# Softmax shift of half the head units on TensorE, own banks for the last pair, and a new step table

## The reference

```python
k, q, v = heads(LN-free context, LN(x), context)       # 16 heads of 8 features
score = einsum('bhij,bhkj->bhik', k, q) / sqrt(8)
attn = softmax(score, axis=1)                          # over the 16 heads
x = x + tanh(g) * (einsum('bhik,bhij->bhjk', attn, v) ... @ Wo.T + bo)
x = x + tanh(g) * moe(LN(x))                           # 8 experts of 256, top 2, silu(x w0) * (x w1) @ wo
z = concat([c, c2q, c * c2q, c * q2c]) @ W_l.T + b_l   # second attention, c = LN(x), q = context
x = x + tanh(g) * z
x = x + tanh(g) * bitlinear_ffn(LN(x))                 # 128 -> 512 -> 128, gate, up and down
```

## Time and profile before

| what | us |
|---|---|
| median of 3 runs (lowest, highest) | 435.32 (432.39, 439.3) |
| the profiled execution | 432.61 |
| its span | 430.8 |
| busy PE, DVE, POOL, ACT | 317.4, 328.7, 285.2, 238.5 |

### The profile page before, as it was taken

One profiled execution on the slowest core, in us unless ns is written; L12 is line 12 of the kernel. 1 busy time (PEld: TensorE's weight loads), 2 busy tenths in 40 slices (PEclk: granted clock), 3 DMA queues, 4 the chain that ended last, 5 costly groups with the idle time before them and its releaser, 6 DMA issues. The chain is left out here.

```text
span 430.8 us, 9908 instructions
## 1 busy us (share of the span) xinstructions
PE 317.4 (74%) x3106; PEld 275.4 (64%) x3106; DVE 328.7 (76%) x1003; ACT 238.5 (55%) x630; POOL 285.2 (66%) x440
## 2 busy tenths in 40 slices
PE   0133348889888888898998898878879978984622
PEld 0122236778787777777887797768768867873501
DVE  1467445968778999999899989997989877785233
ACT  3503314534574679468847865785558647645434
POOL 4145877788889698789869897888686934231100
PEclk9999999999899999999999999999999999996555
DMA  5672410430141024003400430034000100100000
GB/s 169 187 201 71 115 59 2 118 92 2 41 123 48 2 68 138 6 0 88 135 4 2 124 97 2 2 98 114 3 11 2 38 2 2 38 2 1 12 0 12
DMA packets 34214, 24.03 MB, mean 56 GB/s; under 512 B 3570, under 2 KB 31860, under 8 KB 34164
## 3 DMA queue, kind: packets, MB, share of 16 engines
q1 hardware_dynamic: 33444, 23.22, 18.9%
q10 hardware_dynamic: 720, 0.20, 0.2%
HBM read 16.07 MB, written 7.34 MB: 54 GB/s over the span
## 5 line engine op out<-in xcount | busy, mean ns | idle before, releaser
L816 PE MATMUL ps_z<-m_xhi,w_hi 128*128 128x256 f32 x256 | 81.1, 317 | 14.9 <-DVE m_h L1141 8.3
L620 POOL TENSOR_TENSOR attn<-attn,head_inv 128x1024 f32<-128x1024 f32 x32 | 75.7, 2369 | 2.3 <-DVE head_inv L1116 2.3
L698 ACT ACTIVATE m_tanh<-ps_z 128x256 f32<-128x256 f32 x128 | 48.6, 383 | 46.7 <-PE ps_z L818 46.6
L817 PE MATMUL ps_z<-m_xhi,w_lo 128*128 128x256 f32 x256 | 73.2, 286 | 0.0
L1009 PE MATMUL ps_d<-wdn,m_h 128*128 128x128 f32 x512 | 70.8, 281 | 3.3 <-DVE m_h L1141 1.3
L818 PE MATMUL ps_z<-m_xlo,w_hi 128*128 128x256 f32 x256 | 73.1, 285 | 0.0
L1009 PEld LDWEIGHTS ps_d<-wdn,m_h 128*128 128x128 f32 x512 | 62.2, 191 | 6.7 <-issue 3.0
L567 POOL TENSOR_TENSOR m_h<-m_u,m_z 128x256 f32<-128x256 f32 x56 | 41.1, 735 | 37.6 <-DVE m_u L1133 37.6
L1133 DVE SCALAR_TENSOR_TENSOR m_u<-m_tanh,ps_z 128x256 f32<-128x256 f32 x128 | 53.1, 415 | 15.0 <-ACT m_tanh L698 13.4
L816 PEld LDWEIGHTS ps_z<-m_xhi,w_hi 128*128 128x128 f32 x256 | 49.5, 193 | 22.1 <-DVE m_u L1133 8.7
L614 POOL TENSOR_TENSOR tree<-tree 128x256 f32<-128x256 f32 (+2 forms) x96 | 48.5, 505 | 7.5
(11 more groups left out here) (205 smaller groups left out, 762.2 us busy)
## 6 DMA issues: line engine op xcount, KB each, us to landing
rows_dram<-qk_parts SPq DMA_DIRECT2D x16, 192.0 KB, 2.1
k_rows<-rows_dram SPq DMA_DIRECT2D x16, 192.0 KB
q_rows<-rows_dram SPq DMA_DIRECT2D x16, 192.0 KB
w_raw<-in_w SPq DMA_DIRECT2D x2, 1024.0 KB, 6.8
rows_dram<-qk_parts SPq DMA_DIRECT2D x16, 128.0 KB, 1.8
x_in<-in_x SPq DMA_DIRECT2D x8, 128.0 KB, 2.2
ct_in<-in_ctx_t SPq DMA_DIRECT2D x8, 128.0 KB, 2.3
rows_dram<-qk_parts SPq DMA_DIRECT2D x16, 64.0 KB, 1.9
```

The source lines that it names most:

```text
L620: pool.tensor_tensor(e, e, head_inv[:, u % 2].unsqueeze(1).to_broadcast([P, HEADS, HALF]), ALU.mult).then_inc(s_attn, 1)
L698: act.activation(m_tanh[:, k % 2], ps_z[k % 2][:, 0:TOK], ACT.Tanh, scale=0.5).then_inc(s_mt, 1)
L816: pe.matmul(dst, hi_w, hi_x, start=start, stop=False)
L817: pe.matmul(dst, lo_w, hi_x, start=False, stop=False)
```

## The change

The step table gets one time for each step and pair (`WHEN`), and the set-up of weights becomes steps of their own (`ONCE`). In units 1 and 3 of every pair (`PE_UNITS`) the shift goes to PE: after the maximum, ACT and DVE split it in a high and a low part of 128x64, PE multiplies them by minus the identity into both banks of `ps_sc` (four matmuls of 512 columns, each part read as 8 copies), and computes the scores a second time on top; ACT takes the exponential right from `ps_sc`. In the first pair two units sum their heads by one DVE reduction (`SUM_DVE`). The biases are three bf16 parts on partitions 0, 32 and 64, prepared once. `ct_hi`, `ct_lo`, `g_tanh` and `g_u` have two buffers. The k projection comes before the transposes of x. The products `f_z` are two steps; in the last pair the second batch's go to `ps_a`, each `g_up` unit has its own bank, and the second batch's transposes and `g_down` go to `ps_d`. The high parts of w0 and w1 are made in halves, as four steps on ACT.

```diff
+PE_UNITS = {c: (1, 3) for c in range(PAIRS)}
+SUM_DVE = {0: (1, 3)}
...
-AT = {
...
+WHEN = {
...
+    "act.head_exp": (
+        (3054, 4586, 8813, 12724, 16993, 21416, 25795, 29771),
+        (3472, 5674, 9409, 13197, 17725, 22127, 26137, 30164),
...
+ONCE = {
...
+    "sp.w_late": 1568,
...
+    "act.w_hi": (1447, 1218, 2951, 1351),
...
-                    if c == 0:
-                        when += place(FIRST, step, n)
-                    if c == PAIRS - 1:
-                        when += place(LAST, step, n)
...
+        if step.startswith(engine + "."):
+            for n, when in enumerate(at if isinstance(at, tuple) else (at,)):
+                steps.append((when, step, n, 0))
     return [(step, n, c) for _, step, n, c in sorted(steps)]
+
+
+def sums(c, u, dve):
+
...
+def units(c, u, pe):
+
+    return sum((b in PE_UNITS[a]) == pe for a in range(c + 1) for b in range(4) if (a, b) <= (c, u))
...
+                if due(now, "sp.w_late"):
+                    sp.dma_start(wdn[:], A["wdn"].rearrange("n (t p) e -> p (n t) e", p=P)).then_inc(w_late, 16)
+                    sp.dma_start(wl[:], A["wl"].rearrange("(k d) o -> d k o", d=P)).then_inc(w_late, 16)
...
-                        if p.first and n == 1:
-                            last_weights()
...
+                for k in range(4):
+                    if due(now, "act.w_hi", k):
+                        n, half = k % 2, slice((k // 2) * HALF_W, (k // 2 + 1) * HALF_W)
+                        act.wait_ge(w_moe, 48)
+                        act.activation(w01_hi[:, n, half], w01_raw[:, n, half],
+                                       ACT.Copy).then_inc(c_hi1 if n else c_hi0, 1)
...
+                    if (p := due(now, "act.head_hi", u)) and u in PE_UNITS[p.c]:
+                        act.wait_ge(s_hmax, p.count(4, u + 1))
+                        wait(act, s_less, units(p.c, u, True) - 1)
+                        act.activation(max_hi[:], head_max[:, u % 2], ACT.Copy).then_inc(s_mxh, 1)
                     if p := due(now, "act.head_exp", u):
                         b, k0 = u // 2, HALF * (u % 2)
-                        act.wait_ge(s_shift, p.count(4, u + 1))
+                        src = shifted[:, u % 2]
+                        if u in PE_UNITS[p.c]:
+                            act.wait_ge(s_less, units(p.c, u, True))
+                            src = ps_sc[:].rearrange("p a (h k) -> p (a h) k", k=HALF)
...
                         wait(act, s_pv, p.before().count(2, b + 1))
-                        act.activation(attn[:, b, :, k0:k0 + HALF], shifted[:, u % 2], ACT.Exp).then_inc(s_exp, 1)
+                        act.activation(attn[:, b, :, k0:k0 + HALF], src, ACT.Exp).then_inc(s_exp, 1)
...
-                        wait(act, s_guu, p.count(4, u))
-                        act.activation(g_tanh[:], ps_g[:, 0:256], ACT.Tanh,
+                        wait(act, s_guu, p.count(4, u - 1))
+                        act.activation(g_tanh[:, u % 2], unit_bank(p, u)[:, 0:256], ACT.Tanh,
...
+            def wait_bank(eng, p, u):
+
+                q, u = (p, u - 1) if u else (p.before(), 3)
+                if q.c < 0:
+                    return
+                if u in PE_UNITS[q.c]:
+                    eng.wait_ge(s_exp, q.count(4, u + 1))
+                else:
+                    eng.wait_ge(s_shift, units(q.c, u, False))
+
...
+                        wait_bank(pe, p, u)
...
+                    if (p := due(now, "pe.scores_less", u)) and u in PE_UNITS[p.c]:
...
+                        b, k0 = u // 2, HALF * (u % 2)
...
+                        pe.wait_ge(s_mxl, units(p.c, u, True))
+                        for hq in range(2):
+                            for part in (max_hi, max_lo):
+                                top_of = part[:].unsqueeze(1).to_broadcast([P, HEADS // 2, HALF])
+                                pe.matmul(ps_sc[:, hq].rearrange("p (h k) -> p h k", k=HALF), minus_id[:], top_of,
+                                          start=(part is max_hi), stop=False)
+                        scores(b, k0, start=False).then_inc(s_less, 1)
...
+                    pe.wait_ge(s_rest[0], p.count(1, 1))
...
-                    pe.wait_ge(s_axlo, p.count(1, 1))
...
                 if p := due(now, "pe.kq", 1):
-                    pe.wait_ge(s_rest[0], p.count(1, 1))
+                    pe.wait_ge(s_axlo, p.count(1, 1))
...
-                        pe.matmul(ps_a[:, s], ones[0:1], bv_row[:], start=True, stop=False)
...
+                        pe.matmul(ps_a[:, s], ones_bf[:], bias_parts[:, 0], start=True, stop=False)
...
-                if p := due(now, "pe.f_z"):
+                if p := due(now, "pe.f_z", 0):
+                    pe.wait_ge(s_fc2, p.count(1, 1))
+                    pe.wait_ge(s_fq2, p.count(1, 1))
...
+                    if not p.after():
+                        pe.wait_ge(s_x1, p.count(2, 2))
+                    for b in range(1 if p.after() else 2):
+                        s = slice(b * P, (b + 1) * P)
+                        pe.matmul(z_bank(p, b)[:, s], f_ct[:, s], wl[:, 0], start=True, stop=False)
+                        pe.matmul(z_bank(p, b)[:, s], f_c2q[:, s], wl[:, 1], start=False, stop=False)
+                if p := due(now, "pe.f_z", 1):
+                    pe.wait_ge(s_fpr, p.count(1, 1))
                     pe.wait_ge(s_fw, p.count(2, 2))
-                    pe.wait_ge(s_fpr, p.count(1, 1))
...
-                        pe.matmul(ps_f[:, s], f_ct[:, s], f_w4[:, b], start=False, stop=False)
...
+                        if b and p.after():
+                            pe.matmul(z_bank(p, b)[:, s], f_ct[:, s], wl[:, 0], start=True, stop=False)
+                            pe.matmul(z_bank(p, b)[:, s], f_c2q[:, s], wl[:, 1], start=False, stop=False)
+                        pe.matmul(z_bank(p, b)[:, s], f_prod[:, s], wl[:, 2], start=False, stop=False)
+                        last = pe.matmul(z_bank(p, b)[:, s], f_ct[:, s], f_w4[:, b], start=False, stop=True)
...
+                        if p.after():
+                            wait(pe, s_gp, p.count(4, u))
+                        elif u < 2:
+                            pe.wait_ge(s_exp, p.count(4, 4))
+                        else:
+                            wait_product(pe, p, TILES - 4 + u)
                         for n in range(2):
-                            last = pe.matmul(ps_g[:, 256 * n:256 * (n + 1)], g_qt[:, b * P:(b + 1) * P],
+                            last = pe.matmul(unit_bank(p, u)[:, 256 * n:256 * (n + 1)], g_qt[:, b * P:(b + 1) * P],
                                              wf_q[:, n, c0:c0 + 256], start=True, stop=True)
                         last.then_inc(s_gu, 1)
...
+                            pe.wait_ge(s_gqs, p.count(1, 1))
+                        else:
+                            pe.wait_ge(s_y, p.count(2 * EXPERTS, 2 * EXPERTS))
...
-                        pe.matmul(ps_a[:, 0:P], ones[0:1], bo_row[:], start=False, stop=True).then_inc(s_res, 1)
+                        pe.matmul(ps_a[:, 0:P], ones_bf[:], bias_parts[:, 1], start=False, stop=True).then_inc(s_res, 1)
...
+                    if (p := due(now, "dve.head_lo", u)) and u in PE_UNITS[p.c]:
+                        n = units(p.c, u, True)
+                        dve.wait_ge(s_mxh, n)
+                        wait(dve, s_less, n - 1)
+                        dve.tensor_tensor(max_lo[:], head_max[:, u % 2], max_hi[:].bitcast(F32),
+                                          ALU.subtract).then_inc(s_mxl, 1)
+                    if (p := due(now, "dve.head_shift", u)) and u not in PE_UNITS[p.c]:
...
+                    if (p := due(now, "dve.head_sum", u)) and u in SUM_DVE.get(p.c, ()):
+                        b, k0 = u // 2, HALF * (u % 2)
+                        dve.wait_ge(s_exp, p.count(4, u + 1))
+                        wait(dve, s_hinv, p.count(4, u - 1))
+                        e = attn[:, b, :, k0:k0 + HALF]
+                        dve.tensor_reduce(tree[:, u % 2, 14], e.rearrange("p h k -> p k h"), AX.X,
+                                          ALU.add).then_inc(s_hsum, 1)
                     if p := due(now, "dve.head_inv", u):
```

662 lines of the change are left out of this document (421 added, 241 removed), and 148 rows, old and new, of the table WHEN.

## The result

| | before | changed |
|---|---|---|
| median of 5 runs, us | 435.3 | 444.49 |
| lowest to highest, us | 432.39 to 439.3 | 443.3 to 449.44 |
| ratio | | 1.0247 [1.0201, 1.0293] |
| profiled execution; span, us | 432.6; 430.8 | 449.44; 446.9 |
| start, to the first `m_xhi`, us | 72.1 | 76.5 |

The account below looks back on a forecast made before the run. The prediction took DVE to bound the middle, with PE close behind. From 432.6 us it took 8.5 (start), 6 (middle) and 2.9 (end), giving 415.2, and added 0.8 for the median: 416 us, range of 8 in 10 405 to 428.

Parts of the forecast that it names:

- So DVE bounds it, with PE close behind: Middle, steady pair of 40.9 us: DVE, busy 38.8 us, sets the time; PE is busy 36.4 us.
- the middle's -6 us: Seven intervals between the eight m_xhi: 1.0 us saved per pair, counted in six; bounds 0 and -13 us.
- Read as load, a pair could shrink by only 0.3 us; read as DVE's slack, by 1.9: Middle: two readings of the saving per pair, as PE becomes busiest; 1.0 us was taken in between.
- 4.5 us idle: Middle: PE's idle time in a steady pair, expected to take the change's +2.1 us of PE work.
- hand-offs block the in-order engines: Rival, each pair from unit's maximum to scores_less: slower, 454 us in full, chance 0.05; in part 428 to 442, 0.05.
- Start: -8.5 forecast: Stretch up to the first m_xhi: earlier q and less POOL work save 8.5 us, between -3 and -12.
- The first term, q ahead of the copies: Start: q's parts go ahead of most w0 and w1 copies, first scores at about 28.5 us; 4.4 us saved.
- the third rival: Start: wdn and wl delay the fetch, first scores stay at 32.9 us; 420 us in all, chance 0.07.
- POOL's term: Start: two head-sum trees move from POOL to DVE, at about 1.22 us each there; 4.1 of 5.5 us counted.
- The forecast of 1.57 us: PE's added work per PE unit: 0.96 us for four 512-column matmuls, 0.61 for the second scores.
- the banks' term: End: own banks free the four g_up units from waiting for g_p, 9.0 us become 6.5; -2.5 us.
- the -0.7 and +0.3 for `f_z` and `x3`: End: four f_z products moved ahead save 0.7 us; x3 as two instructions adds about 0.3 us.

Follow-up runs that it names:

- e5: Kernel before, with DVE's subtraction in units 1 and 3 of pairs 2 to 8 cut to one head of 16: 433.40 us, ratio 0.996.
- e10: Kernel before, with the third product left out of 13 of 16 up tiles, so less PE work: 433.62 us, ratio 0.9977.
- e16: Kernel before, with e10's cut of PE work and e14's filler matmuls together: 433.16 us, ratio 0.9989.
- e17: e16 with e5's cut of DVE's subtraction too, so both engines have less work: 433.34 us, ratio 0.9999.
- e1: Kernel before, with only PE work added ahead of the scores of units 1 and 3 (four wide matmuls, scores once more): 448.68 us, ratio 1.0355.
- e6: e2 with DVE's subtraction in units 1 and 3 of pairs 2 to 8 cut to one head of 16: 433.76 us, ratio 0.9977.
- e7: Changed kernel with the first pair's four units shifted by DVE again, the other seven pairs as changed: 439.29 us, ratio 1.0104.
- e3: Changed kernel with all hand-offs kept, but PE's four wide matmuls and second scores replaced by two matmuls of 64 columns: 432.68 us, ratio 0.9959.
- e9: Kernel before in its old order, with the PE units added in pairs 2 to 8, without new banks and biases: 455.80 us, ratio 1.0487.
- e8: Changed kernel with the transfers wdn and wl issued behind the fetches of q_rows, as before: 445.45 us, ratio 1.0241.
- e2: Changed kernel with no PE units, all four units shifted by DVE, the rest of the change kept: 444.22 us, ratio 1.0231.
- e11: Changed kernel with ten small bf16 filler matmuls ahead of the first up tile's wait for m_xlo in each pair: 437.73 us, ratio 1.0063.
- e13: Changed kernel with the edits of e7 and e11 together: 433.86 us, ratio 0.9985.
- e14: Kernel before with the filler matmuls of e11: 432.18 us, ratio 0.9917.
- e12: Kernel before, old order, with the last pair's own g_up banks, two tanh and u buffers, and the bf16 biases: 431.05 us, ratio 0.9922.

## Why the prediction was wrong

**The step that failed is "So DVE bounds it, with PE close behind".** From it came the middle's -6 us, and "Read as load, a pair could shrink by only 0.3 us; read as DVE's slack, by 1.9". Both readings price a pair by the busiest engine. Load taken from DVE (e5), from PE (e10, e16) or from both (e17) changes no more than 0.4% of the time, and a steady interval of each with the clock at 1.00 takes 40.6 to 40.9 us, while load added to PE ahead of the scores costs 0.59 of itself (e1). My reading, which no run shows, is that a chain across the engines in their written orders sets a pair: up tile on PE, tanh on ACT, `m_u` on DVE, `m_h` on DVE or POOL, then the bank for the next up tile. What the waits show fits it: taken load turns into a wait (the 11.7 us of `m_u` for tanh, and `m_h` on PE in e10); added load stands in front of the next tile. Which one cycle of waits closes at 41 us was not settled: no run shortened it.

**The middle's counts were right by instruction, not by engine.** The groups of the shift lost 13.5 us over seven pairs (forecast 13), but DVE's busy time fell from 38.8 to 38.3 us in a steady pair, not to 36.9. PE +18.2 us, 2.6 per pair (forecast 2.1, bounds 0.5 to 3.1). What I counted as harmless, +2.1 us on "4.5 us idle", is the cost: from e6 to e7 (the hand-offs and PE's work, pairs 2 to 8) +5.5 us, and from e3 to the changed kernel (PE's work alone, all pairs) +11.8; as e3 and e6 can't be told apart, the 5.5 are put down to PE's work. The rival "hand-offs block the in-order engines" had the sign, at a chance of 0.05 in full and 0.05 in part, and in the new order not the mechanism: the distances in the order covered the hand-offs, as argued. In the old order (e9) this isn't shown.

**Start: -8.5 forecast, +4.4 measured.** The first term, q ahead of the copies, is there in full only with e8's edit (first scores 28.92; I said 28.5), because the third rival held in the change itself. It bought nothing even then: the term assumed that the first scores set the first `m_xhi`, and ACT's wait for the next pair's `ct_in` stands behind them (e8). POOL's term is partly there: without PE units in pair 1 (e7) the first weighted values start at 46.86 us instead of 50.10, 3.2 of the 4.1 us, but the first `m_xhi` comes only 1.5 us earlier (70.6; in e2 2.9). DVE's head sum took 1.88 us, not 1.22. So a start of -8.5 us was wrong by 5.6 to 7.0 us before any PE unit. The rest is pair 1's PE units: I counted their work and who waits for `max_lo`, and not that the second scores read `k_rows` and `q_rows` again, so that SP's fetch waits for `s_less`. It stands in the change as a wait on SP; with the longer chain of the units it costs 5.2 us (e7; 3.9 from e11 to e13).

**The price of a PE unit: a mean of two speeds.** The forecast of 1.57 us adds 0.96 for four matmuls from a stretch at the upper level and 0.61 for the scores from the start. Where the granted clock is 1.00 the four start 0.24 us apart and a unit takes 1.4 us (110.18 to 111.54), by which e1's load is 22 us and its share 0.66. In the start they stand 0.43 apart, and the unit holds the buffers for 2.6 us (51.09 to 53.70). The column PEclk doesn't tell this: it reads 1.00 in the start, but its first entry in the trace of the changed kernel is at 86.0 us (before: 76.2), and up to there 256-column matmuls stand 0.21 us apart, as they do at 0.50, and 0.12 from there on:

```profile
85.52 0.41 PE L1117 MATMUL ps_z<-m_xhi,w_lo 128*128 128x256 f32 x1
85.74 0.41 PE L1118 MATMUL ps_z<-m_xlo,w_hi 128*128 128x256 f32 x1
85.95 0.32 PE L1116 MATMUL ps_z<-m_xhi,w_hi 128*128 128x256 f32 x1
86.11 0.28 PE L1117 MATMUL ps_z<-m_xhi,w_lo 128*128 128x256 f32 x1
86.22 0.28 PE L1118 MATMUL ps_z<-m_xlo,w_hi 128*128 128x256 f32 x1
```

So the 1.00 of the first line of the earlier trace rows is no reading of the clock. (`wdn` and `wl` carry 1.31 MB, not 1.25; nothing hangs on it.)

**The clock was no term at all.** In the earlier trace rows it is 1.00 in the steady pair, and I took it as given. The new order leaves PE waits of 1.4 to 1.9 us right ahead of each of the four falls: for `m_xlo`, for `m_xn`, for `f_ctq`, and one at 99.7 us for which the trace names no releaser. There are 24 us at the lower level in the middle. The order brings them and not PE's work: e2 and e6, the new order without it, have a granted clock of 0.94 over the middle, some 35 us at the lower level. Within the 91 runs of the kernel before, 1 us more at the lower level goes with 0.28 us more time, which would make some 6 us of the 20; that is an estimate from runs that go together, and no run sets the clock alone. It doesn't carry over to every kernel: within the few runs of others the figure lies between 0.0 (e1) and 0.6 (e2), and of the changed kernel's five runs the longest, 449.44, has the highest clock (0.928; the others 0.912 to 0.914). Nor is it what the filler gives back: e14 gains 3.6 us at an unchanged clock, and e11 is faster at the same clock too. How much of the 10.6 us is the clock is open.

**End: the banks' term was right, the sum past its bound.** -4.5 us against -2.9, half a microsecond past its bound of -4. From the end of `x3` to the last record 20.1 us instead of 22.8, -2.7 against -2.5. The chain of the changed kernel (start, us, what), which answers to the earlier trace rows:

```profile
433.19 1.05 PE ps_sc L1303 x4
434.26 0.48 ACT g_tanh L1093
...
435.10 0.88 DVE g_p L1687 x2
436.00 0.70 DVE g_pmax L1692
...
437.53 0.15 DVE g_u L1681
437.86 0.88 DVE g_p L1687 x2
```

The four products of the first unit stand at 433.19, and no later `g_up` is in the chain: DVE runs on from 435.10, as the step said. The other 1.8 us lie in the last pair's MoE stage, which I had not priced: from `m_xhi` to the last `y` 29.6 us instead of 31.4. The f stage behind it, up to the end of `x3`, takes 21.1 us in both, so the -0.7 and +0.3 for `f_z` and `x3` don't show.

**What this makes of the sum.** By the ratios and times above: with banks, biases, the new order and DVE's relief, but none of PE's work, the kernel stands 1.0 us below before (e6). PE's work of pairs 2 to 8 adds 5.5 (e7), pair 1's units 5.2: together +9.7, measured +10.6. That it comes out is no proof, since the steps lead from one kernel to the other; it divides the change. As banks and biases alone give -3.4 (e12), the new order with DVE's relief is itself a loss of some 2.4 us, about as much as the two intervals leave open.

## What to carry to other kernels

Where engines hand tiles round in a written order, busy shares of 95% and 89% may name no bound: before an edit is costed at "slack", try which engine's work, taken away alone, moves the interval. Here added work cost and removed work paid next to nothing. An operand read a second time keeps its buffer until then: look for the transfer that waits for that buffer, above all in the first pair. Price a matmul by the distance of the starts in the stretch where it will stand, not by a clock column that has no entry there, and look for the waits of PE that the new order leaves.

## What the runs showed of the hardware

- Ten needless bf16 matmuls (0.73 us of PE) ahead of a wait made the changed kernel 6.8 us faster and the kernel before 3.6 us (by the ratio), in eight places each; the profiled clock of the middle rose in the first (0.96 to 1.00) and stayed at 0.99 in the second.
- The same 512-column fp32r matmuls start 0.24 us apart where the granted clock is 1.00 (from 110 us on) and 0.43 in the start; 256 columns 0.12 at 1.00, 0.21 at 0.50 and in the start.
- A `tensor_reduce` of DVE from 128x1024 to 128x64 takes 1.22 us as `head_max` (maximum, from `ps_sc`) and 1.88 us as a head sum (from `attn`). Whether the operation, the memory or the stride makes the difference was not tried.
- `max_lo`, 128x64, took 0.20 to 0.26 us in 13 of 16 times, as forecast, and 0.41, 0.59 and 0.71 us in three, the last while POOL's `head_norm` ran. That POOL is the cause isn't shown:

```profile
47.69 2.34 POOL L906 TENSOR_TENSOR attn<-attn,head_inv 128x1024 f32<-128x1024 f32 x1 [2.17 <-DVE head_inv L1519]
...
49.40 0.71 DVE L1496 TENSOR_TENSOR max_lo<-head_max,max_hi 128x64 fp32r<-128x64 f32 x1 [0.32 <-ACT max_hi L996]
```
